# Rotary attention without permuted projections: the rotation on GpSimd, q, k and v evacuated by ScalarE, and stack stores of 128 rows

## What is computed

```python
def rot(x):
    xp = x.reshape(B, H, N, d // 2, 2)
    xx, xy = (xp[..., 0], xp[..., 1])
    rx = xx * cos - xy * sin
    ry = xx * sin + xy * cos
    return jnp.stack([rx, ry], axis=-1).reshape(B, H, N, d)
q = (x @ Wq.T + bq).reshape(B, N, H, d).transpose(0, 2, 1, 3)
k = (x @ Wk.T + bk).reshape(B, N, H, d).transpose(0, 2, 1, 3)
q, k = _rope(q, k)
scores = jnp.einsum('bhnd,bhmd->bhnm', q, k) / jnp.sqrt(jnp.asarray(d, x.dtype))
out = jnp.einsum('bhnm,bhmd->bhnd', jax.nn.softmax(scores, axis=-1), v)
```

## Time and profile before

| | |
|---|---|
| runs | 2465.03, 2466.25, 2470.92 us |
| profiled execution, its own time | 2471.75 us |
| its span, first to last instruction | 2470.0 us |
| granted TensorE clock, mean | 0.94 of full |
| TensorE busy | 2097.5 us (85%) |
| VectorE busy | 1723.2 us (70%) |
| ScalarE busy | 1482.2 us (60%) |
| GpSimd busy | 982.3 us (40%) |
| first maxima of attention b | 1219.30 us from the start |

### The profile page before, as it was taken

One profiled execution on the slowest core, in us unless ns is written; L12 is line 12 of the kernel. 1 busy time (PEld: TensorE's weight loads), 2 busy tenths in 40 slices (PEclk: granted clock), 3 DMA queues, 4 the chain that ended last, 5 costly groups with the idle time before them and its releaser, 6 DMA issues. The chain is left out here.

```text
span 2470.0 us, 37314 instructions
## 1 busy us (share of the span) xinstructions
PE 2097.5 (85%) x13378; PEld 971.9 (39%) x13378; DVE 1723.2 (70%) x2590; ACT 1482.2 (60%) x2980; POOL 982.3 (40%) x1184
## 2 busy tenths in 40 slices
PE   0799999999985999998378898989898885999998
PEld 0233333333322777776112222222222112777776
DVE  5677777777643667664388889888988843666663
ACT  0166666666662655655037777777777773655655
POOL 2355555555421544544322332233323101554544
PEclk8599999999985999999569999999999997999999
DMA  5535454545310000000433344334433300000000
GB/s 155 108 78 103 83 106 88 105 85 106 67 21 11 1 1 1 1 1 2 101 77 62 68 86 87 68 67 88 85 70 65 64 16 11 9 9 14 13 10 18
DMA packets 99853, 136.48 MB, mean 55 GB/s; under 512 B 20560, under 2 KB 81488, under 8 KB 93520
## 3 DMA queue, kind: packets, MB, share of 16 engines
q1 hardware_dynamic: 99664, 134.02, 26.0%
HBM read 67.91 MB, written 55.57 MB: 50 GB/s over the span
## 5 line engine op out<-in xcount | busy, mean ns | idle before, releaser
L577 DVE TENSOR_REDUCE b_negmax<-ps_max 128x2 f32<-128x1024 f32 x512 | 614.2, 1221 | 92.9 <-PE ps_max L695 91.5
L662 ACT ACTIVATE b_prob<-ps_score 128x512 f32<-128x512 f32 x1024 | 545.8, 599 | 206.7 <-PE ps_score L681 205.5
L662 ACT ACTIVATE a_prob<-ps_score 128x512 f32<-128x512 f32 (+3 forms) x1024 | 384.0, 437 | 226.0 <-PE ps_score L681 224.0
L577 DVE TENSOR_REDUCE a_negmax<-ps_max 128x2 f32<-128x256 f32 (+3 forms) x512 | 411.4, 822 | 150.1 <-PE ps_max L699 142.6
L681 PE MATMUL ps_score<-b_stack_q,stack_k 50*128 50x512 bf16 x1024 | 258.8, 387 | 56.8 <-ACT b_prob L662 48.3
L716 PE MATMUL ps_out<-b_prob,b_v_aug 128*9 128x512 f32 x2048 | 268.6, 596 | 17.7 <-ACT b_o_raw L635 11.6
L978 PE MATMUL ps_score<-fb_h,w_hi 128*128 128x512 f32 x1024 | 252.0, 401 | 29.7 <-DVE fb_h L892 28.7
L978 PE MATMUL ps_score<-fa_h,w_hi 128*128 128x512 f32 x1024 | 251.4, 400 | 29.7 <-DVE fa_h L892 28.7
L494 POOL TENSOR_SCALAR_AFFINE_SELECT a_prob<-a_prob 128x512 f32<-128x512 f32 x256 | 162.0, 635 | 276.8 <-ACT a_prob L662 276.8
L695 PE MATMUL ps_max<-stack_k,b_stack_q 48*128 48x512 bf16 x1024 | 231.1, 397 | 27.1 <-DVE b_negmax L577 17.3
L681 PEld LDWEIGHTS ps_score<-b_stack_q,stack_k 50*128 50x128 bf16 x1024 | 63.9, 93 | 417.8 <-ACT b_prob L662 337.3
(11 more groups left out here) (139 smaller groups left out, 2877.1 us busy)
## 6 DMA issues: line engine op xcount, KB each, us to landing
stack_k<-d_stack SPq DMA_DIRECT2D x64, 384.0 KB, 6.0
d_stack<-a_parts SPq DMA_DIRECT2D x64, 192.0 KB, 2.8
a_stack_q<-d_stack SPq DMA_DIRECT2D x32, 384.0 KB, 5.7
d_stack<-b_parts SPq DMA_DIRECT2D x64, 192.0 KB, 2.8
b_stack_q<-d_stack SPq DMA_DIRECT2D x32, 384.0 KB, 5.6
d_stack<-a_parts SPq DMA_DIRECT2D x64, 128.0 KB, 2.8
d_stack<-b_parts SPq DMA_DIRECT2D x64, 128.0 KB, 2.8
d_stack<-a_parts SPq DMA_DIRECT2D x64, 64.0 KB, 2.5
```

Of the source, the lines that this page charges most:

```text
L577: dve.tensor_reduce(m["negmax"][:, t, :, p], dve_banks("max", k)[:, :, 0:keys], AX.X, ALU.max, negate=True).then_inc(s["max"], 1)
L662: act.activation(m["prob"][u % PROBS][:, g, lo:S], act_bank("score", 4 * u + g)[:, 0:S - lo], ACT.Exp).then_inc(s["prob"], 1)
```

## The change

In stage b:
- The rows of q and k are ordered with all even features ahead of all odd ones (`rows_of_heads`). Row r and row r+64 are then the two partners of a rotation, and the permuted projections qr and kr, their weights and biases are gone.
- ScalarE evacuates q and k with their bias (`flat`, into `qf`) and v without one, from banks of its own turns. GpSimd multiplies the 64 rows of either half by the signed sine into the other half of `turned` (two instructions), multiplies `qf` by the cosine, and adds. It adds v's bias when it copies v.
- VectorE has none of q, k, v any more. Its turns are 33 a step, filled up to 34; ScalarE's are 70, filled up to 72.
- The slots are k 0, nm1 2, v 4, proj 6, xT 9, nm0 10, q 12.

In both attention stages:
- A store is three DMAs of 128 rows in place of six of 64; the scratch tensor is laid out by part and row.
- A load reads the 48 rows as 12 blocks of 4. The loads of each of the three stacks have a semaphore of their own.
- Four weight matrices are loaded in place of six. The slots of stage a stay.

The diff, cut to its core:

```diff
-        m["d_stack"] = dram("d_stack", (2, 2, 2, TERMS, HD, PAIRS, S), BF16)
+        m["d_stack"] = dram("d_stack", (2, 2, TERMS, P, S), BF16)
...
+    by_act = ("nm1", "nm0", "xT") + (("q", "k", "v") if rotary else ())
     act_turns, dve_turns = [], []
     for u in range(UNITS):
         act_turns += [("score", 2, 4 * u + g) for g in range(4)]
         dve_turns += [("max", 1, 2 * u), ("max", 1, 2 * u + 1)]
-        for name, lag in (("nm1", 2), ("nm0", 1), ("xT", -1)):
-            if SLOT[name] == u:
-                act_turns.append((name, lag, 0))
-        for name, lag in (("proj", 4), ("q", -1), ("qr", -1), ("k", 0), ("kr", 0), ("v", 0)):
-            if SLOT[name] == u and (rotary or name not in ("qr", "kr")):
-                dve_turns.append((name, lag, 0))
+        for name, lag in (("nm1", 2), ("nm0", 1), ("xT", -1), ("proj", 4), ("q", -1), ("k", 0), ("v", 0)):
+            if slot[name] == u:
+                turns = act_turns if name in by_act else dve_turns
+                turns.append((name, lag, 0))
...
-                for o in range(2):
-                    parts = m["parts"][64 * o:64 * (o + 1), i]
-                    rows = m["d_stack"][b % 2, i, o].rearrange("t d p n -> (d p) t n")
-                    for part, (lo, hi) in enumerate(((0, 3), (3, 5), (5, 6))):
-                        held = parts[:, part:part + 1].broadcast_to([64, hi - lo, S]) if i == 0 else parts[:, 0:hi - lo]
-                        sp.dma_start(rows[:, lo:hi], held).then_inc(s[name], 16)
+                rows = m["d_stack"][b % 2, i].rearrange("t r n -> r t n")
+                for part, (lo, hi) in enumerate(((0, 3), (3, 5), (5, 6))):
+                    held = m["parts"][:, i, part:part + 1].broadcast_to([P, hi - lo, S]) if i == 0 \
+                        else m["parts"][:, i, 0:hi - lo]
+                    sp.dma_start(rows[:, lo:hi], held).then_inc(s[name], 16)
...
-                    sp.dma_start(m[name][b % STACKS][rows], m["d_stack"][b % 2, i, o].rearrange("t d p n -> (t d) p n"))\
-                        .then_inc(s[name], 16)
+                    held = m["d_stack"][b % 2, i].rearrange("t (e o d p) n -> o (t e) d p n", e=2, o=2, p=PAIRS)
+                    sp.dma_start(m[name][b % STACKS][rows], held[o])\
+                        .then_inc(s[f"{name}{b % STACKS}"], 16)
...
+            def rotated(n, b, name, i):
+                if name == "k":
+                    if on(n, 2):
+                        pool.wait_ge(s["nm"], count(2, n - 2, 2))
+                    else:
+                        pool.wait_ge(s["parts"], count(2, b, 1))
+                elif on(n, 1):
+                    pool.wait_ge(s["nm"], count(2, n - 1, 1))
+                else:
+                    pool.wait_ge(s["rstd"], b + 1)
+                pool.wait_ge(s[f"{name}_flat"], b + 1)
+                flat, turned, rope = m["qf"][:, i], m["turned"][:, i], m["rope"]
+                for to, of in ((0, SIDE), (SIDE, 0)):
+                    last = pool.tensor_tensor(turned[to:to + SIDE], flat[of:of + SIDE],
+                                              rope[of:of + SIDE, 2 * i + 1], ALU.mult)
+                last.then_inc(s[f"{name}_turn"], 1)
                 pool.wait_ge(s[f"{name}_turn"], b + 1)
+                pool.tensor_tensor(flat, flat, rope[:, 2 * i], ALU.mult).then_inc(s[f"{name}_main"], 1)
                 pool.wait_ge(s[f"{name}_main"], b + 1)
-                pool.tensor_tensor(m["qf"][:, i], m["qf"][:, i], m["turned"][:, i], ALU.add).then_inc(s[name], 1)
+                pool.tensor_tensor(flat, flat, turned, ALU.add).then_inc(s[name], 1)
...
-                pool.wait_ge(s["v"], b + 1)
+                pool.wait_ge(s["v_flat" if rotary else "v"], b + 1)
...
+                if rotary:
+                    bias = m["bias_row"][:, 0:1, :].rearrange("p o (h d) -> p o h d", h=H).broadcast_to([P, T, H, HD])
+                    pool.tensor_tensor(to[:, :, :, 0:HD], v, bias, ALU.add).then_inc(s["v_aug"], 1)
+                    return
...
-                if not rotary:
-                    dve.tensor_scalar(m["qf"][:, i], bank, m["bias_col"][:, i:i + 1],
-                                      1.0 if i else SCALE, ALU.add, ALU.mult).then_inc(s[name], 1)
-                    return
-                dve.scalar_tensor_tensor(out=m["qf"][:, i], in0=bank, scalar=m["bias_col"][:, i:i + 1],
-                                         in1=m["rope"][:, 2 * i], op0=ALU.add, op1=ALU.mult)\
-                    .then_inc(s[f"{name}_main"], 1)
-            def turn(b, name, i):
-                dve.wait_ge(s[f"{name}r_ps"], b + 1)
-                wait(dve, s[name], b)
-                dve.scalar_tensor_tensor(out=m["turned"][:, i], in0=dve_banks(name + "r")[:, 0],
-                                         scalar=m["bias_col"][:, 2 + i:3 + i], in1=m["rope"][:, 2 * i + 1],
-                                         op0=ALU.add, op1=ALU.mult).then_inc(s[f"{name}_turn"], 1)
...
+            def flat(b, name, i):
+                act.wait_ge(s[f"{name}_ps"], b + 1)
+                wait(act, s["parts"], count(2, b, i - 1))
+                act.activation(m["qf"][:, i], act_bank(name), ACT.Identity, bias=m["bias_col"][:, i:i + 1])\
+                    .then_inc(s[f"{name}_flat"], 1)
...
+                    if rotary and u == slot["q"] + 1 and on(n, -1):
+                        flat(n + 1, "q", 0)
+                    if rotary and u == slot["k"] + 1 and on(n, 0):
+                        flat(n, "k", 1)
+                    if rotary and u == slot["v"] + 1 and on(n, 0):
+                        act.wait_ge(s["v_ps"], n + 1)
+                        wait(act, s["v_aug"], n)
+                        act.activation(m["v"][:].rearrange("p t d -> p (t d)"), act_bank("v"), ACT.Copy)\
+                            .then_inc(s["v_flat"], 1)
...
+                    pe.wait_ge(s[f"stack_q{c}"], count(LOADS, b // STACKS, LOADS))
+                    pe.wait_ge(s[f"stack_k{c}"], count(LOADS, b // STACKS, LOADS))
...
-                    if rotary and u == SLOT["qr"]:
-                        linear(n, n + 1, "qr", W_QR)
...
-                if rotary and u == SLOT["kr"]:
-                    linear(n, n, "kr", W_KR)
...
-SLOT = {"k": 0, "nm1": 1, "kr": 2, "v": 4, "proj": 6, "xT": 9, "nm0": 10, "q": 11, "qr": 13}
+SLOT = {"a": {"k": 0, "nm1": 1, "v": 4, "proj": 6, "xT": 9, "nm0": 10, "q": 11},
+        "b": {"k": 0, "nm1": 2, "v": 4, "proj": 6, "xT": 9, "nm0": 10, "q": 12}}
...
-    return np.array([(2 * p + o) * HD + d for o in range(2) for d in range(HD) for p in range(PAIRS)])
+    return np.array([(2 * p + o) * HD + 2 * d + e for e in range(2) for o in range(2) for d in range(HD // 2)
+                     for p in range(PAIRS)])
...
-    sin = np.where((d % 2 == 0)[:, None], -sin, sin)
+    sin = np.where((d % 2 == 1)[:, None], -sin, sin)
```

More of the change, by code:

```diff
@@ L224, in attention @@
     m["xT"] = sb("xT", [P, S])
-    m["weights"] = sb("weights", [P, 6, P])
-    m["bias_col"] = sb("bias_col", [P, 4])
+    m["weights"] = sb("weights", [P, 4, P])
+    m["bias_col"] = sb("bias_col", [P, 2])
     m["bias_row"] = sb("bias_row", [P, 2, D])
@@ L246, in attention @@
     m["oT"] = sb("oT", [P, S])
-    W_Q, W_K, W_V, W_QR, W_KR, W_O = range(6)
+    W_Q, W_K, W_V, W_O = range(4)
+    slot = SLOT[tag]
     def width(j):
@@ L338, in _ @@
         def _(sp):
-            sp.dma_start(m["weights"][:, 0:6, :], w["w"].rearrange("n k m -> k n m")).then_inc(s["loads"], 16)
+            sp.dma_start(m["weights"][:], w["w"].rearrange("n k m -> k n m")).then_inc(s["loads"], 16)
             sp.dma_start(m["bias_col"][:], w["bias_col"]).then_inc(s["loads"], 16)
@@ L516, in _ @@
                     for i, (name, lag) in enumerate((("q", -1), ("k", 0))):
-                        if on(n, lag) and u == SLOT[name + "r" if rotary else name] + 1:
+                        if on(n, lag) and u == slot[name] + 1:
                             if rotary:
-                                rotated(n - lag, name, i)
+                                rotated(n, n - lag, name, i)
                             high(n - lag, name, i)
-                        if on(n, lag) and u == SLOT[name + "r" if rotary else name] + 2:
+                        if on(n, lag) and u == slot[name] + 2:
                             middle_low(n - lag, i)
-                    if u == SLOT["nm0"] - 1 and on(n, 1):
+                    if u == slot["nm0"] - 1 and on(n, 1):
                         negated_max_parts(n - 1, 0)
@@ L586, in _ @@
                             norm_apply(dve, m, s, n + 1)
-                        if u == SLOT["q"] + 1:
+                        if causal and u == slot["q"] + 1:
                             project(n + 1, "q", 0)
-                        if rotary and u == SLOT["qr"] + 1:
-                            turn(n + 1, "q", 0)
-                    if on(n, 0):
-                        if u == SLOT["k"] + 1:
+                    if causal and on(n, 0):
+                        if u == slot["k"] + 1:
```

(24 more changed lines are left out.)

47 lines of the change are left out of this document (24 added, 23 removed).

## The result

The changed kernel takes 2503.9 us (median of 4 runs, 2499.99 to 2509.99); the kernel before took 2465.64 us in the same comparison (4 runs). The ratio is 1.0152, with a 95% interval from 1.0135 to 1.0169. The forecast was 2447.2 us, faster than before by 19.0 us; the change is slower by 38.3, so the sign was wrong.

What follows compares the result with a forecast made beforehand. It took a TensorE-ScalarE ring, VectorE close behind, to bound steady b, and VectorE b's half-clock first step. Terms 0.1 + 1.3 - 5.3 - 14.3 - 0.8 = -19.0 us gave 2447.2 us from the median, range 2432 to 2463.

Steps and rivals of the forecast that it cites:

- the part on GpSimd: GpSimd in steady b: chain grows from 5.1 to 8.9 us, with no one waiting; numerators land near 14.7, needed near 15.8.
- In the steady state no long wait is on a load, so nothing: SP's queue in the steady state: 3 stores for 6 with the same bytes change the time by nothing.
- The steady step: Steps 2 to 14 of stage b: unit-by-unit savings of 1.10 us a step, 13 x 1.10 = -14.3 us.
- the prediction's terms: Stage b: -14.3 us for steps 2 to 14, -0.8 for step 15, -5.3 for step 1.
- The first step of b at half clock: Step 1 of b, bound by VectorE: removed projections and evacuations save 5.3 us, bounds 2 and 6.
- The rival of a late GpSimd at v: ScalarE waiting before v's evacuation: slower GpSimd additions give 3.6 us of stall, +2.5 a step, 2497 us; chance 0.08.
- ScalarE's ring: Rival in steady b: three ScalarE evacuations each cost their full 0.6 us, +0.8 a step, 2473 us; chance 0.10.
- the stores: Stage a prologue: half the store issues but the same data save 0.9 of the 1.9 us of issue.
- the load: Prologue stack loads: 12 blocks of 4 use fewer engines and cost +1.4 us, bounds 0 and +2.2.
- The first maxima of a: Stage a prologue: -0.4 for weights, -0.9 for stores and +1.4 for loads make +0.1 us.
- The stage b prologue as a whole: Start of b: a longer GpSimd k chain and slower load cost +1.3 us, bounds 0 and +5.8.

Runs made afterwards that it cites:

- the one-buffer version with another order: Changed kernel with SP's numerator loads ahead of the k stack's load and GpSimd's output product ahead of k's rotation, one `o_raw` kept: 2443.52 us, ratio 0.9907.
- the version with two buffers in both stages: Changed kernel with a second `o_raw` buffer for the group outputs in both attention stages: 2452.22 us, ratio 0.9931.

## Why the prediction was wrong

**The step that failed** is the one in the part on GpSimd: that the numerator loads "land near 14.7 (maxima at 6.2, their row at 7.6, then 5.1 of issues, [...] and an estimated 2 to land), and the evacuation that needs them comes near 15.8". The evacuation asked at 16.0. The numerators were there at 18.15. The 3.45 us between forecast and fact have two parts:

- *Issue, 1.0.* The same paragraph puts the output product at 10.2, behind k's chain, and the order of GpSimd's instructions ahead of the prediction shows it there. SP's numerators wait for that product. I followed who waits for the chain's end and for v, and not who waits for the product. The issues ended at 13.7, not at 12.7: 0.7 of it is the wait for the product (1528.41 to 1529.13), the rest the issues' own length.
- *Landing, 2.5.* I took 2 us as an estimate without a row. The trace of the kernel before had one. Its numerators are issued in the row below, and their last completion write comes at 1531.23:

```profile
1524.75 3.16 SPq L364 DMA_DIRECT2D b_o_num<-b_o_raw  x4
```

From the end of the last issue to the last completion write the median over 11 steps of b is 3.2 us in the kernel before, where SP's next store follows 2.2 to 3.9 us later. It is 4.4 us in after, and 4.3 to 4.5 in the five experiments in which the 128-row stores of k follow as in after, 0.04 us behind. With stores of 64 rows as close behind it is 3.3, and with those of 128 rows about 2 us behind (the transposed maxima in slot 1 and the product first) it is 3.3 too. So the 3.2 of the old kernel alone, in place of 2, would have put the landing at 15.9 and used up the spare time; the 128-row stores right behind add about 1.1. "In the steady state no long wait is on a load, so nothing" was wrong about stores too: with nobody waiting for them, they delay what others wait for.

With 1.1 us to spare by my own numbers, this wait should have been a rival with a price, as the one on GpSimd and v (1.5 to spare) was. It would have been on the slower side: 3.4 us of loss against 1.1 of gain in each step. In the profile that is 25.1 us between the first and last maxima of b (45.5 lost by the wait, 20.4 gained).

**A mis-sized cost.** A stall was priced at its length. Here 2.2 us of wait cost 3.4: behind 2.65 us of an idle TensorE the clock is at half for 3.4 us, and the eight matmuls that come first take 1.89 us for 1.04.

**Right:**
- The steady step: -1.10 us predicted, 48.5 for 49.5 measured as soon as the wait is gone, in four kernels. From the first to the last maxima of b the prediction's terms give 787.2 - 14.3 - 0.8 - 5.3 = 766.8 us; the one-buffer version with another order took 766.8. That it agrees to the tenth is luck, for the other three without the wait took 765.4 to 768.0. The rest of its gain (5.5 us in the maxima of a, 3.9 behind them) was not predicted.
- The first step of b at half clock: 43 us predicted, 43.1 measured (43.1 or 43.2 in the eight experiments with its slots of k, v and q).
- GpSimd: k's high part at 9.2 us for 8.9, its low part at 13.4 for 13.3, 1.26 to 1.29 us for each 64-row multiply (two in 2.58), no wait of ScalarE for v's copy in the steady state. The rival of a late GpSimd at v has the right side and the wrong waiter: no operation of GpSimd was slower than taken, and nobody waited for v in the steady state. Its own sum, 2497, came nearer to the result than the forecast, by luck.
- ScalarE's ring (ScalarE and TensorE waiting for each other) doesn't pay for the evacuations: units 1, 5 and 13 stand at 3.11 to 3.15.

**Mis-sized, both small.** The DMA queue, VectorE and TensorE in the prologues, for the earlier trace rows:

```profile
58.51 1.57 SPq L396 DMA_DIRECT2D d_stack<-a_parts  x3
62.21 1.57 SPq L405 DMA_DIRECT2D stack_k<-d_stack  x2
```

```profile
1205.77 1.71 SPq L396 DMA_DIRECT2D d_stack<-b_parts  x3
1209.49 1.57 SPq L405 DMA_DIRECT2D stack_k<-d_stack  x2
```

```profile
1216.93 1.04 PE L723 MATMUL ps_max<-stack_k,b_stack_q 48*128 48x512 bf16 x4 [3.51 <-DMA stack_k<-d_stack]
```

Store to load is 3.7 us in place of 5.7, so the stores give 2.0 and not 0.9. Load to first use is 7.44 us in place of 7.05, so the load costs 0.4 and not 1.4. The Trainium skill (DMA: Bandwidth & Descriptors, section "Why a DMA increments its semaphore by 16 and not by 1") is right on the number: the trace has 12 completion writes for such a load where it had 16. The time I drew from it isn't there. The first maxima of a end 1.9 us earlier than before, where 0.1 later was predicted. The stage b prologue as a whole, from the last `fa_tanh` to the first maxima, grew by 2.3 us against 1.3 predicted. One slip of arithmetic in its upper bound changed nothing: 3 x 1.27 twice, less 1.9, is 5.7 and not 5.8.

**Open.** 10 us of the loss lie behind the last maxima of b (82.0 for 71.5 us). The two stretches, first before, then after:

```profile
2010.00:2080.00 70.00, 38.54 (x232) 11.73 (x232) 7.98 (x31) 35.83 (x70) 4.16 (x6) 0.82 0.10 18
```

```profile
2033.00:2113.00 80.00, 47.96 (x232) 12.16 (x233) 7.98 (x31) 35.93 (x69) 3.80 (x4) 0.71 0.09 16
```

The work is the same and the clock is lower. The stretch takes 71 to 73 us in six of the eleven experiments' traces and 80 to 82 in five, and the five are not those with the wait (the version with two buffers in both stages has 80.2). I can't say what chooses, nor whether the change makes the longer one more frequent. It may make up much of the spread between the runs of one kernel, but no run shows that, since each kernel has a single trace.

## What to carry to other kernels

When a step moves back on one engine, list every semaphore that its instructions set and what stands in each queue behind the waits on them. Here the product was moved behind a chain, a DMA queue waited for the product, ScalarE for the DMA, and TensorE for ScalarE. Give a DMA's landing a row of the trace, look at what is issued right behind it, and where a single buffer ties an evacuation to it, treat spare time of about a microsecond as none. Then compare the price of a second buffer with that of the order: both cured it here, and the order did it without memory.

## What the runs showed of the hardware

- A short idle time of TensorE is dearer than its length. Behind 2.65 us of idle the clock was at half for 3.4 us, and a step lost 3.4 us for a wait of 2.2. Behind about 1.7 us of idle (64-row stores) it still fell so in nine of 13 steps. With 4.2 us of wait on ScalarE it was at half for 6.8 us in 11 of 12 steps, and a step lost 6.1.
- Loads whose 48 rows come as 12 blocks of 4 lose little by their fewer engines: in the two prologues their packets of 8 KB took 541 and 548 ns in the mean in place of 720 and 764, and from issue to first use the load lost 0.3 and 0.4 us.
- The stores of 128 rows are quicker for their bytes (packets of 1 KB took 46 ns in the median between 1300 and 1900 us, before 73) and a worse neighbour: small loads issued just ahead of them landed 4.4 us after their issue, against 3.3 with stores of 64 rows there and 3.2 with none close behind.
- A multiply on 64 partitions takes GpSimd 1.26 us; an addition on 128 takes 1.27.
